# One ScalarE copy for a head's eight transposed blocks instead of two, and TensorE waiting for the whole of it

## The chip, the cores and the metric

The kernel runs on one core of a Trainium2 chip. The metric is the device time of one launch in microseconds; smaller is better. One core has five engines that run their own instruction streams in order and meet only at semaphores: TensorE (PE, with PEld for its weight loads), VectorE (DVE), ScalarE (ACT), GpSimd (POOL) and SyncE (SP), which issues the DMAs.

## The reference

A four-stage layer stack on `x` of shape (8, 1024, 256), in float32. The change touches the first stage alone:

```python
def _L0_attn_ref(hidden_states, ...):          # on layernorm(x); H = 16 heads of hd = 16
    q = (x @ Wq.T + bq).reshape(b, s, h, hd)   # k, v alike
    attn_scores = jnp.einsum('bihd,bjhd->bhij', q, k) / scale
    li = x @ rel_W[:, :d].T
    lj = x @ rel_W[:, d:].T
    relation_probs = jax.nn.softmax(li[:, :, None, :] + lj[:, None, :, :] + rel_b, axis=-1)
    bias = jnp.einsum('bijk,hk->bhij', relation_probs, logical_bias)
    attn_scores = attn_scores + gate * bias
    attn_weights = jax.nn.softmax(attn_scores, axis=-1)
    out = jnp.einsum('bhij,bjhd->bihd', attn_weights, v).reshape(b, s, d)
    return out @ Wo.T + bo
```

The three stages behind it (a matrix product with fp8 weights, a Mamba block with its scan and MLP, a gated FFN) are not touched.

## The kernel before

Attention goes over 64 tiles of 128 queries (8 batches of 8 tiles, `TILES`), and in each tile over 16 heads (`H`). It takes place from about 200 us to about 3470 us of the trace. The order on every engine is written out by hand: each engine has a `body` that runs once for a tile `t`, with a loop over `u` = 0..15 inside. A semaphore that counts heads uses `U = 16 t + h`.

For head `u` of a tile the steps are these.

- `dve_f` (L315, twelve heads) or `pool_f` (L225, L227; heads 4, 8, 12 and 15) builds the relation bias of the head in one of eight row buffers `srow`.
- `pe_s` (L469) computes the 128x1024 scores into PSUM (`ps_s`, one buffer). It waits until VectorE is done with the head before (`s_ok`).
- `dve_s` (L326) adds bias and scores, leaves the result in `srow`, and finds the row's extremum; it gives `s_ok`.
- `act_e` (L398) takes the exponential of the 128x1024 row on ScalarE.
- `pe_t` (L480) transposes the eight 128x128 blocks of the head `u - 2` (`LAG` is 2) into PSUM tile `ps_t`, which has two halves of four blocks: 2 KB each for a partition, 4 KB together, and no second buffer.
- `act_at` (L407) copies `ps_t` into `AT` in SBUF, in two instructions of 128x512, one for each half.
- `pe_pv` (L492) multiplies `AT` with the values, for groups of four heads, in three pieces at u % 4 = 3, 0 and 1.

The wait pairs around `ps_t` go by halves. TensorE may write half 0 of the next head as soon as half 0 of this one has been copied, and ScalarE may copy half 0 as soon as four transposes are done.

Beside the heads, a tile carries the work of its neighbours at fixed places of the loop over `u`. On ScalarE in `body`: after the copy of u = 1, 4 and 5 the exponentials of the next tile's relation terms (`act_rel`, L381 and L385), at u = 5 `act_o` (L411, the output accumulator for `pe_oT`), at u = 7 `act_gate` (L375), at u = 8 `act_xT` (L345), at u = 9 `act_y0` (L391, a logarithm, and L393, an exponential of its result), at u = 11 `act_d` (L349, L352), at u = 15 `act_p` (L361). The output of `act_y0` goes to GpSimd (`pool_t`, L212), and its result to VectorE (`dve_y`, L303) at u = 11, which sits in VectorE's queue ahead of the heads 12 to 15. On TensorE at u = 5 there is `pe_v` (L457), at u = 6 `pe_oT` (L502; VectorE's `dve_norm`, L332, waits for it), at u = 7 `pe_xT` (L427), at u = 9 `pe_d` (L444), at u = 10 `pe_g` (L450).

In what follows T(h) is the eight transposes of head h, copy(h) the copy or the two copies of `act_at` for head h, and exp(u) the exponential of `act_e`. At step u ScalarE issues exp(u), copy(u - 2), and then the extra work; TensorE issues the scores of head u + 1, T(u - 2), the piece of `pe_pv`, and then the extra work.

Of the kernel before, what the change touches and what calls it, by code (L numbers as in the profile page):

```python
# [21 lines left out]
H = 16  # L22
HD = D // H
HG = 4
# [7 lines left out]
def wait(eng, sem, value):  # L32

    if isinstance(value, int) and value <= 0:
        return
    eng.wait_ge(sem, value)
# [10 lines left out]
def attention(nc, x_in, wqk, wvg, bqk, rows, ident_in, parts_d, x_out):  # L47
# [6 lines left out]
    NROW = 8  # L54
# [6 lines left out]
    NAT = 2 * HG  # L61
    with ExitStack() as ctx:
# [54 lines left out]
        AT = [sb(f"AT{i}", [P, NT, P]) for i in range(NAT)]  # L117
# [9 lines left out]
        ps_t = psum("ps_t", [P, 2, HG, P])  # L127
# [45 lines left out]
        t_ok = sem("t_ok")  # L173
# [227 lines left out]
        def act_at(act, t, h):  # L401
            U = H * t + h
            if h % HG == 0:
                wait(act, pv_ok, U // HG + 1 if isinstance(U, int) else HG * t + h // HG + 1)
            for half in range(2):
                wait(act, t_ok, 2 * NROW + 2 * U + half + 1)
                nc.scalar.copy(AT[h % NAT][:, HG * half:HG * half + HG, :], ps_t[:, half]).then_inc(at_ok, 1)  # L407

        def act_o(act, o):
            wait(act, pv_ok, 2 + HG * (o + 1))  # L410
# [62 lines left out]
        def pe_t(pe, t, h):  # L473
            U = H * t + h
            wait(pe, e_ok, U + 1)
            for half in range(2):
                wait(pe, at_ok, 2 * U + half + 1)
                for i in range(HG):
                    j = HG * half + i
                    last = nc.tensor.transpose(ps_t[:, half, i, :], rows_sb[h % NROW][:, j * P:(j + 1) * P], ident[:])  # L480
                last.then_inc(t_ok, 1)

        def pe_pv(pe, t, par, j, blocks):
            if blocks[0] == 0:
                if j == 0:
                    wait(pe, o_ok, t)
                    wait(pe, v_ok, 2 + NT * (t // NT + 1))
                wait(pe, at_ok, 2 + 2 * (H * t + HG * j + HG))
            for n in blocks:
                for i in range(HG):  # L490
                    h = HG * j + i
                    last = nc.tensor.matmul(ps_o[32 * i:32 * i + 32, j, :], V[par][:, n, h, :],  # L492
                                            AT[h % NAT][:, n, :], start=(n == 0), stop=(n == NT - 1))
            if blocks[-1] == NT - 1:
                last.then_inc(pv_ok, 1)
# [316 lines left out]
        @block.scalar  # L812
        def _(act):
            def front(act, p):
                act_xT(act, p)
                act_d(act, p)
                act_hi(act, p)
                act_mid(act, p)

            def project(act, p, k, par, ib):  # L820
                act_xT(act, p)
                act_d(act, p)
                act_hi(act, p)
                act_gate(act, p, par, ib)
                act_mid(act, p)

            def start(act):
                front(act, NT)
                for step in range(3):
                    act_rel(act, 0, 0, step)  # L830
                act_y0(act, 0)
                act_p(act, 0, 0)

            def body(act, t, k, par, ib, pro, post, look, before):
                for u in range(H):
                    act_e(act, t, u)
                    if u >= LAG:
                        act_at(act, t, u - LAG)
                    elif post:
                        act_at(act, t - 1, H + u - LAG)  # L840
                    if followed(t, pro) and u == 0:
                        act_hi(act, t - 1 + AHEAD)
                    if u == 0 and (not isinstance(t, int) or t >= 2):
                        act_aT(act, t - 2)
                    if look and u in (1, 4, 5):
                        act_rel(act, t + 1, 1 - k, (1, 4, 5).index(u))
                    if followed(t, pro) and u == 3:
                        act_mid(act, t - 1 + AHEAD)
                    if post and u == 5:
                        act_o(act, t - 1)  # L850
                    if pro and u == 7:
                        act_gate(act, t + NT, 1 - par, ib)
                    if pro and u == 8:
                        act_xT(act, t + AHEAD)
                    if look and u == 9:
                        act_y0(act, t + 1)
                    if pro and u == 11:
                        act_d(act, t + AHEAD)
                    if look and u == 15:
                        act_p(act, t + 1, 1 - k)  # L860

            def finish(act):
                for u in range(H - LAG, H):
                    act_at(act, TILES - 1, u)
                act_aT(act, TILES - 2)
                act_o(act, TILES - 1)
                act_aT(act, TILES - 1)

            act.preload_act_table_set("natural_log_exp_and_others")
            act.sem_inc(at_ok, 2)  # L870
            run(act, start, project, body, finish)

        @block.tensor
# [1018 lines left out]
```

## Time and profile before

| | us |
|---|---|
| median of 3 runs | 7194.83 |
| the runs | 7194.24 to 7202.27 |
| the profiled execution | 7195.28 |
| its span in the trace | 7193.3 |
| TensorE busy | 5460.0 (76%) |
| VectorE busy | 5274.5 (73%) |
| ScalarE busy | 3797.2 (53%) |
| GpSimd busy | 4038.8 (56%) |

The span runs from the first to the last instruction of the trace; 2.0 us of the execution lie around it. The busy shares are means over four stages with different limits, so for the change only the attention stage counts. The page's slices are 180 us each; attention fills the second to the nineteenth.

### The profile page before, as it was taken

What the parts mean: (1) busy time and instruction counts of PE and PEld (TensorE: products, weight loads), DVE (VectorE), ACT (ScalarE), POOL (GpSimd) and SP (SyncE); (2) the same over time, 40 slices, a digit from 0 to 9 for tenths busy, and PEclk for the clock granted to TensorE, in tenths of its full rate; (3) what the DMA queues carried; (4) which work ended last, traced back from release to release, by engine and by line L of the source; (5) the groups of instructions that cost most, each with busy time, mean ns of one, the idle gap of its engine ahead of it and who ended that gap; (6) DMA issues with size and microseconds to landing.
All of it is one profiled execution on the core that took longest, in us unless ns stands there. A gap on an engine that the chain in (4) does not pass through costs nothing. (4 is left out here: it accounts for less than half of the span.)

```text
span 7193.3 us, 118342 instructions
## 1 busy us (share of the span) xinstructions
PE 5460.0 (76%) x36898; PEld 3382.9 (47%) x36898; DVE 5274.5 (73%) x6522; ACT 3797.2 (53%) x5385; POOL 4038.8 (56%) x2175
## 2 busy tenths in 40 slices
PE   4688888888888888877535667667666666999999
PEld 3466565656665665655322222222222223666665
DVE  1788888888888888888776998998988986121221
ACT  1788888888888888888313333333333332111111
POOL 2777676767776777766223766866865864000000
PEclk7899999999999999999767988888888888999999
DMA  1212121110212021110223343443443434101110
GB/s 36 35 28 40 27 41 26 35 32 23 44 24 44 23 43 24 29 30 14 68 97 108 140 144 118 149 138 120 147 144 112 155 132 136 44 29 44 29 44 9
DMA packets 401678, 486.09 MB, mean 68 GB/s; under 512 B 225936, under 2 KB 303504, under 8 KB 401184
## 3 DMA queue, kind: packets, MB, share of 16 engines
q1 hardware_dynamic: 401184, 479.68, 22.9%
q8 instruction: 289, 4.73, 0.3%
q14 instruction: 205, 1.68, 0.1%
HBM read 394.25 MB, written 85.33 MB: 67 GB/s over the span
## 5 line engine op out<-in xcount | busy, mean ns | idle before, releaser
L1391 PE MATMUL c_ps_y<-c_hc,c_ident 128*128 128x512 f32 x2048 | 1127.3, 698 | 680.8 <-POOL c_hc L1417 326.4
L326 DVE CUSTOM_DVE_ANT_0 srow<-srow,ps_s,cur 128x1024 f32<-128x1024 f32 x1024 | 1304.8, 1274 | 317.3 <-PE ps_s L469 271.2
L1410 POOL TENSOR_TENSOR c_db<-c_conv,c_bs 128x1024 f32<-128x1024 f32 x512 | 1221.6, 2415 | 502.1 <-DVE c_conv L1536 411.1
L398 ACT ACTIVATE srow<-srow,nmax 128x1024 f32<-128x1024 f32 x1024 | 1186.6, 1159 | 279.8 <-DVE nmax L326 269.4
L407 ACT COPY AT<-ps_t 128x512 f32<-128x512 f32 x2048 | 1110.6, 594 | 248.4 <-PE ps_t L480 246.6
L1445 ACT ACTIVATE c_pd<-c_dt,c_a_neg 128x1024 f32<-128x1024 f32 x512 | 571.6, 1117 | 1140.4 <-DVE c_hc L1555 1011.1
L480 PE MATMUL ps_t<-ident,srow 128*128 128x128 f32 x8192 | 1136.4, 284 | 18.0 <-ACT AT L407 17.6
L480 PEld LDWEIGHTS ps_t<-ident,srow 128*128 128x128 f32 x8192 | 1000.5, 146 | 279.3 <-ACT AT L407 68.7
L469 PE MATMUL ps_s<-K,Q 96*128 96x512 bf16 x2048 | 645.9, 398 | 602.0 <-DVE nmax L326 519.0
L1391 PEld LDWEIGHTS c_ps_y<-c_hc,c_ident 128*128 128x128 f32 x2048 | 423.5, 220 | 1389.8 <-issue 510.8
L1546 DVE TENSOR_TENSOR_SCAN c_pd<-c_pd,c_db 128x1024 f32<-128x1024 f32 x384 | 876.5, 2283 | 0.0
L315 DVE SCALAR_TENSOR_TENSOR srow<-ps_p,rho,R 128x1024 f32<-128x1024 f32 x640 | 817.9, 1278 | 0.8 <-ACT ps_p L361 0.8
L227 POOL TENSOR_TENSOR srow<-srow,R 128x1024 f32<-128x1024 f32 x256 | 642.4, 2509 | 47.0 <-POOL srow L225 47.0
L492 PE MATMUL ps_o<-AT,V 128*32 128x128 f32 x16384 | 660.2, 295 | 0.0
L469 PEld LDWEIGHTS ps_s<-K,Q 96*128 96x128 bf16 x2048 | 145.1, 99 | 801.7 <-DVE nmax L326 687.8
L1694 POOL TENSOR_TENSOR d_rstd<-d_ve,d_mhalf 128x4 f32<-128x4 f32 x16 | 16.3, 1019 | 898.7 <-DVE d_ve L967 898.7
L492 PEld LDWEIGHTS ps_o<-AT,V 128*32 128x32 f32 x16384 | 433.8, 116 | 146.6 <-issue 141.6
L1555 DVE TENSOR_TENSOR c_hc<-c_pd,c_cs 128x1024 f32<-128x1024 f32 x384 | 470.1, 1224 | 13.3
L1417 POOL TENSOR_TENSOR c_hc<-c_hs,c_cs 128x1024 f32<-128x1024 f32 x128 | 300.1, 2344 | 183.4 <-DVE c_hs L1546 182.4
L200 POOL TENSOR_TENSOR R<-Dj,RT 128x1024 f32<-128x1024 f32 x128 | 300.7, 2371 | 101.3 <-DVE RT L298 101.3
L217 POOL TENSOR_TENSOR R<-R,R 128x1024 f32<-128x1024 f32 x128 | 300.4, 2367 | 92.1 <-DVE R L303 92.1
L1721 DVE TENSOR_TENSOR d_x<-d_ps_y,d_y 128x512 f32<-128x512 f32 x32 | 22.1, 692 | 438.3 <-PE d_ps_y L1796 438.3
(180 smaller groups left out, 8166.3 us busy)
## 6 DMA issues: line engine op xcount, KB each, us to landing
c_bs<-bc_rows_d SPq DMA_DIRECT2D x256, 512.0 KB, 4.8
c_cs<-bc_rows_d SPq DMA_DIRECT2D x256, 512.0 KB, 4.1
parts_d<-parts SPq DMA_DIRECT2D x65, 384.0 KB, 3.3
K<-parts_d SPq DMA_DIRECT2D x192, 128.0 KB, 4.5
Q<-parts_d SPq DMA_DIRECT2D x384, 64.0 KB, 2.9
ym_d<-c_conv SPq DMA_DIRECT2D x32, 512.0 KB, 2.9
d_ym<-ym_d SPq DMA_DIRECT2D x16, 1024.0 KB, 7.3
xt<-in_x SPq DMA_DIRECT2D x65, 128.0 KB, 3.2
```

Source lines behind the costliest of these rows:

```text
L227: nc.gpsimd.tensor_tensor(r[:], r[:], R[k][0][:], ALU.add).then_inc(fp_ok, 1)
L315: nc.vector.scalar_tensor_tensor(r[:], p1[:], rho[:, h:h + 1], R[k][0][:], ALU.mult, ALU.add).then_inc(fd_ok, 1)
L326: nc.vector.tensor_tensor_reduce(r[:], r[:], ps_s[:], cur[k][:, h:h + 1], BIG, ALU.add, ALU.min, nmax[:, h % NROW:h % NROW + 1]).then_inc( ...
L398: nc.scalar.activation(r[:], r[:], ACT.Exp, scale=-1.0, bias=nmax[:, h % NROW:h % NROW + 1]).then_inc(e_ok, 1)
L407: nc.scalar.copy(AT[h % NAT][:, HG * half:HG * half + HG, :], ps_t[:, half]).then_inc(at_ok, 1)
L469: last = nc.tensor.matmul(ps_s[:, n * 512:(n + 1) * 512], Q6[k][:, h, :], K6[:, h, n * 512:(n + 1) * 512], start=True, stop=True)
L480: last = nc.tensor.transpose(ps_t[:, half, i, :], rows_sb[h % NROW][:, j * P:(j + 1) * P], ident[:])
L492: last = nc.tensor.matmul(ps_o[32 * i:32 * i + 32, j, :], V[par][:, n, h, :], AT[h % NAT][:, n, :], start=(n == 0), stop=(n == NT - 1))
L1391: last = nc.tensor.matmul(ps_y[:, c, cut], ident[:], hc[(2 * n + c) % RING][:, cut], start=n == 0, stop=n == NS - 1)
L1410: nc.gpsimd.tensor_tensor(db[(2 * n + c) % RING][:], conv[:, 2 * pair + c, :], bs[n % RING][:], ALU.mult).then_inc(db_ok, 1)
L1445: nc.scalar.activation(pd[:, c, :], dt[:, m, :], ACT.Exp, scale=a_neg[:, m, n:n + 1]).then_inc(da_ok, 1)
L1546: nc.vector.tensor_tensor_scan(h, pd[:, c, :], db[(2 * n + c) % RING][:], 0.0, ALU.mult, ALU.add).then_inc(h_ok, 1)
```

## The change

ScalarE waits for all eight transposes of a head and copies them with one instruction of 128x1024, where it had two waits and two instructions of 128x512. The semaphore `at_ok` goes up by one for a head where it went up by two. TensorE waits, ahead of the eight transposes of a head, until the whole copy of the head before it is done; before, it waited for half 0 ahead of the first four and for half 1 ahead of the last four. The initial value of `at_ok` and the wait of `pe_pv` are renumbered to match.

```diff
@@ act_at
-            for half in range(2):
-                wait(act, t_ok, 2 * NROW + 2 * U + half + 1)
-                nc.scalar.copy(AT[h % NAT][:, HG * half:HG * half + HG, :], ps_t[:, half]).then_inc(at_ok, 1)
+            wait(act, t_ok, 2 * NROW + 2 * U + 2)
+            nc.scalar.copy(AT[h % NAT][:], ps_t[:].rearrange("p a i t -> p (a i) t")).then_inc(at_ok, 1)
@@ pe_t
             wait(pe, e_ok, U + 1)
+            wait(pe, at_ok, U + 1)
             for half in range(2):
-                wait(pe, at_ok, 2 * U + half + 1)
                 for i in range(HG):
@@ pe_pv
-                wait(pe, at_ok, 2 + 2 * (H * t + HG * j + HG))
+                wait(pe, at_ok, 1 + H * t + HG * j + HG)
@@ block.scalar
-            act.sem_inc(at_ok, 2)
+            act.sem_inc(at_ok, 1)
```

## Rows read from the trace of the kernel before

**Rows 1.** The page: busy time of each engine over the whole span.

```profile
PE 5460.0 (76%) x36898; PEld 3382.9 (47%) x36898; DVE 5274.5 (73%) x6522; ACT 3797.2 (53%) x5385; POOL 4038.8 (56%) x2175
```

**Rows 2.** Busy by windows: from:to us, length, engines, clock, DMA share, GB/s.

```profile
1000.00:1600.00 600.00, 488.27 (x5414) 357.11 (x5416) 504.28 (x708) 499.10 (x748) 430.44 (x257) 0.94 0.17 35
```

**Rows 3.** Waits of 1200 to 1800 us: waiting engine, line, releaser, total us, times, longest.

```profile
DVE srow L326 <- PE ps_s L469: 54.0, 38, 3.1
ACT AT L407 <- PE ps_t L480: 52.0, 53, 3.6
...
PEld ps_t L480 <- ACT AT L407: 13.6, 24, 0.7
```

**Rows 4.** Line L303, whole span: ns min/median/max, and its idle time before.

```profile
L303 DVE SCALAR_TENSOR_TENSOR R<-RT,R x64: 1224/1226/1227, 203.0 to 3403.5; 128x1024 f32<-128x1024 f32 x64
...
  POOL RT L212: 130.4, 64
```

**Rows 5.** Lines L407 and L361, whole span, and who waited for L407.

```profile
L407 ACT COPY AT<-ps_t x2048: 562/589/692, 223.4 to 3459.8; 128x512 f32<-128x512 f32 x187
...
  PEld ps_t L480: 68.7, 116
...
L361 ACT COPY ps_p<-R x64: 1016/1036/1037, 209.0 to 3417.7; 128x1024 f32<-128x1024 f32 x64
```

**Rows 6.** Timeline, a head whose copy waits: start us, us, engine, line, [idle before].

```profile
1504.49 1.04 PE L480 MATMUL ps_t<-ident,srow 128*128 128x128 f32 x8
...
1505.13 1.07 ACT L407 COPY AT<-ps_t 128x512 f32<-128x512 f32 x2 [0.80 <-PE ps_t L480]
```

**Rows 7.** Timeline, the same tile, from T(2) to T(5).

```profile
1509.15 1.01 PEld L480 LDWEIGHTS ps_t<-ident,srow 128*128 128x128 f32 x8
1509.36 1.04 PE L480 MATMUL ps_t<-ident,srow 128*128 128x128 f32 x8
...
1510.00 1.07 ACT L407 COPY AT<-ps_t 128x512 f32<-128x512 f32 x2
...
1510.96 1.16 ACT L385 ACTIVATE R<-R,cur 128x1024 f32<-128x1024 f32 x1
...
1515.05 0.60 ACT L411 COPY O<-ps_o 128x512 f32<-128x512 f32 x1
...
1516.57 1.09 ACT L407 COPY AT<-ps_t 128x512 f32<-128x512 f32 x2
...
1517.22 0.91 PEld L480 LDWEIGHTS ps_t<-ident,srow 128*128 128x128 f32 x8 [0.66 <-ACT AT L407]
```

**Rows 8.** Timeline, the same tile, from copy(5) to `dve_y`.

```profile
1518.56 1.11 ACT L407 COPY AT<-ps_t 128x512 f32<-128x512 f32 x2
...
1519.73 0.11 PEld L469 LDWEIGHTS ps_s<-K,Q 96*128 96x128 bf16 x2 [0.44 <-DVE nmax L326]
...
1519.96 1.01 PEld L480 LDWEIGHTS ps_t<-ident,srow 128*128 128x128 f32 x8
...
1522.35 1.01 PEld L480 LDWEIGHTS ps_t<-ident,srow 128*128 128x128 f32 x8
...
1523.20 1.08 ACT L407 COPY AT<-ps_t 128x512 f32<-128x512 f32 x2
...
1524.16 1.07 ACT L391 ACTIVATE R<-RT 128x1024 f32<-128x1024 f32 x1
...
1526.51 2.37 POOL L212 TENSOR_TENSOR RT<-RT,R 128x1024 f32<-128x1024 f32 x1 [1.60 <-ACT R L393]
...
1528.92 1.23 DVE L303 SCALAR_TENSOR_TENSOR R<-RT,R 128x1024 f32<-128x1024 f32 x1 [1.74 <-POOL RT L212]
```

**Rows 9.** Timeline, a tile of the last batch: T(5), and the first half of `act_y0`.

```profile
3248.17 0.91 PEld L480 LDWEIGHTS ps_t<-ident,srow 128*128 128x128 f32 x8 [0.85 <-ACT AT L407]
...
3255.01 1.07 ACT L391 ACTIVATE R<-RT 128x1024 f32<-128x1024 f32 x1
```

**Rows 10.** Timeline, the end of the same tile as Rows 7, heads 12 and 13 on ScalarE.

```profile
1532.57 1.15 ACT L398 ACTIVATE srow<-srow,nmax 128x1024 f32<-128x1024 f32 x1 [1.43 <-DVE nmax L326]
```

## The prediction

> **What bounds the kernel now.** I read the page first: no engine is busy for more than 76% of the span [rows 1], so the stage has to be read by itself. In a window inside attention TensorE, VectorE, ScalarE and GpSimd are busy for 488, 504, 499 and 430 of 600 us [rows 2]: 81, 84, 83 and 72%. None is full; what sets a tile's time is a chain that passes from engine to engine. The waits say where: over 12 tiles VectorE waits 54.0 us for scores [rows 3]. The view of the line L303 (`dve_y`) shows the other place, and that it is there in every tile: 64 of its 64 instructions came after idle time of VectorE that ended with GpSimd's L212, 130.4 us in all, 2.0 us each [rows 4]. In the timeline L212 in turn sat idle for 1.60 us until ScalarE's L393, the second half of `act_y0`, and the first half, L391, starts on ScalarE with no idle time before it, right behind copy(7) [rows 8]. So one point of ScalarE's queue is on the path of every tile: if ScalarE is late at L391 (u = 9), L212 is late, `dve_y` is late, and so are heads 12 to 15 and the next tile behind it. What has to be found out is how late the change makes L391.
>
> **The change, part by part.** First the prices.
>
> (a) The copy itself. A pair of 128x512 copies that runs without a pause takes 1.07 us, the second starting 0.48 after the first; one lasts 589 ns [rows 5, 6]. A single ScalarE copy of 128x1024 is in the trace only with PSUM on its output side: L361, 1016 ns at least and 1036 at the median [rows 5]. For one that reads PSUM over two halves there is no row. Bounds: 1.02 us, L361's shortest, and 1.18, twice 589 ns, if nothing overlapped. I take 1.03, next to L361's median, since it has the same width and the same two memories. Behind a pair the next instruction starts 0.11 before the end (1510.00 + 1.07 against 1510.96) [rows 7]; so the fused copy takes up 0.92 us of the queue for the pair's 0.96. ScalarE gains about 0.04 us for a head (at the upper bound it loses 0.11).
>
> (b) The later start. Where ScalarE is ready first, the pair starts 0.64 us after the first transpose (1504.49 to 1505.13) [rows 6]. The fused copy needs all eight, which end 1.04 us after that start; with the 0.04 that a semaphore takes, 1.08. It starts 0.44 later and ends 0.40 later. Where ScalarE is more than 0.44 us behind TensorE, this costs nothing.
>
> (c) The later release of `ps_t`. TensorE could load for T(h+1) when half 0 of copy(h) was done, 0.59 us after the start; now at 1.03: 0.44 later. Before, this wait decided in two places of a tile (T(5) and T(9)): 24 waits in 12 tiles, 13.6 us [rows 3], 116 waits in the whole span [rows 5].
>
> (b) and (c) close a ring: 0.21 us from the weight load of T(h) to its first transpose (1509.15 to 1509.36) [rows 7], 1.08 to the copy, 1.03 for the copy, 0.06 to the next weight load (1516.57 + 0.59 = 1517.16 against 1517.22) [rows 7]. 2.38 us for a head, and no other engine can shorten it. The heads in the middle of a tile follow each other at 2.39 us (1519.96 to 1522.35) [rows 8]. By itself the ring doesn't slow them, but it has no reserve: a lag that gets into it stays until a head with slack.
>
> (d) The waits that fall out, one for a head on each of the two engines, I cost at nothing: the second copy followed the first at the width of its data, so the wait had been hidden under it. No DMA is moved, and nothing in SP's queue waits for `at_ok` or `t_ok`. Queued behind TensorE's wait are a piece of `pe_pv`, the extra work and the scores of a later head; behind ScalarE's, its extra work and the next exponential. VectorE's and GpSimd's builders of the bias wait for the transposes of a head eight earlier, which leaves them heads of slack.
>
> Now one tile with these prices.
> 1. copy(2): 1509.36 + 1.08 = 1510.44; exp(4) in front of it, pushed by the later copy(1), ends 0.06 after that. 1510.50 for 1510.00 [rows 7], +0.50; behind it +0.46.
> 2. From there to copy(4) ScalarE is full (L385, exp(5), copy(3), L385, L411, exp(6)), and copy(3) gives back its 0.04: L411 starts 0.44 later [rows 7]. `pe_oT` and `dve_norm` behind it come 0.3 to 0.4 later, and VectorE with them.
> 3. copy(4): 1517.01 for 1516.57, done 1518.04; T(5) is loaded at 1518.10 for 1517.22 [rows 7]: +0.88, half the lag, half (c).
> 4. copy(5): 1518.10 + 0.21 + 1.08 = 1519.39 for 1518.56 [rows 8]: +0.83. By the ring T(6) can be loaded at 1520.48. TensorE's own work from T(5) to T(6) was 2.74 us (1517.22 to 1519.96), 0.44 of it idle ahead of the scores [rows 8]; 2.30, and with some 0.2 of short pauses between weight loads that the idle time hid, 2.5: T(6) at 1520.60 for 1519.96, +0.64.
> 5. T(7) by the ring: 1522.98 for 1522.35 [rows 8], +0.63. copy(7): 1522.98 + 1.29 = 1524.27 for 1523.20, +1.07.
> 6. L391 follows 0.92 later: 1525.19 for 1524.16, +1.03. L212 and `dve_y` wait for it and nothing else [rows 8], so `dve_y` comes 1.03 us later. VectorE's own lateness there (head 11's scores stand behind T(7), 0.64) is covered by its 1.74 us of idle time in front of L303 [rows 8].
> 7. Behind `dve_y`, ScalarE sits idle for 1.43 us before exp(12) [rows 10]: the ring starts empty, and copies that end 0.40 later end in idle time. Nothing is added, and nothing is given back, since the next tile starts from VectorE.
>
> Tiles of the last batch have no projection work, yet T(5) waits for ScalarE there too (0.85 us) and L391 has no idle time before it [rows 9]; the same walk gives about the same. `act_y0` of a next tile is in 63 tiles: 63 x 1.03 = 65 us. Outside attention nothing changes. The profiled execution has 7195.28 us (span 7193.3 and 2.0 around it), 0.45 over the median; so 7260.3 beside it, and against the median **7260 us**, +0.9%.
>
> In heads like that of [rows 6] ScalarE waits 0.80 us for the transposes, and the split lets it begin at the half. The Trainium skill, page "Perfetto Trace Analysis", section "Optimizing Scalar/DVE Operations", has a rule for either side: grouping into larger operations improves throughput if the engine is saturated, and breaking up instructions may let work complete sooner where an unsaturated Scalar or Vector engine causes bubbles on others. By its first half the result would be A below, by its second the forecast.
>
> **The rivals.**
> A. *ScalarE's queue alone decides at L391, and the merger shortens it: faster.* For it: ScalarE has no idle time from copy(2) to L391. If it is always more than 0.44 us behind TensorE, copies 2 to 7 give back 0.04 us each, 0.24 a tile, 15 us: 7180; if a pair really used 2 x 0.59 us, 0.15 each, 0.9 a tile, 57 us: 7138. Against it: ScalarE waited for the transposes 53 times in 12 tiles [rows 3], and T(5) for the copy.
> B. *Covered.* The 2.0 us in front of `dve_y` take the lag: 7195. Against it: that idle time ends with the chain from L391; it is no slack of the chain.
> C. *The copy is at its upper bound.* At 1.18 each of copies 2 to 7 adds 0.15, 0.9, less the 0.1 that TensorE's own work hides at T(6): 1.83 a tile, 115 us: 7310.
> D. *Every head pays (b)*: 16 x 0.44 x 64 = 451 us: 7646. It would need the ring to be slower than VectorE's pace in all heads; [rows 8] and [rows 10] speak against that. In the Trainium skill "Perfetto Trace Analysis", section "Optimizing Tensor Performance", advises that independent matmul groups rotate through PSUM banks so that copying one out overlaps the next; taken for every head it points to D.
> E. *The lag is caught at heads 6 and 7* (TensorE's pauses rearrange), and L391 is late only by (b), 0.40: 25 us, 7220.
>
> **How the numbers follow.** Forecast 0.54, C 0.15, E 0.13, D 0.02, A 0.09, B 0.07. The range reaches from a little under E, 7212, to a little over C, 7315; outside are A, B and D, 0.18. A measurement of this kernel can't tell less than 0.2%, 14 us, from no change. Slower by more: 0.54 + 0.15 + 0.13 + 0.02 = 0.84; within: 0.07; faster: 0.09.
>
> **What would show it.** L407 1024 times at about 1.03 us; TensorE's waits for L407 in more heads than two a tile, over 1 us at T(5) in place of 0.66; weight loads of T(5), T(6), T(7) at least 2.38 us apart; L391 with no idle time before it, and 1 us later counted from copy(2) less its own 0.5; L303's mean idle time 0.4 longer, still ended by L212; the tiles, now (3417.7 - 209.0) / 63 = 50.9 us apart by L361 [rows 5], 51.9 apart. L407 at 1.1 or more would be C; L391 with idle time before it, or L303 released by something else, would make the chain wrong; a wait of TensorE for L407 in nearly every head, D.

## The result and the profile after

The changed kernel took 7261.03 us at the median of 4 runs (7255.17 to 7269.7), the kernel before 7194.53 beside it (7191.02 to 7202.27). The ratio is 1.0092 [1.0077, 1.0107]: slower by 66.5 us (55 to 77). The forecast of 7260 was met, but partly by luck: the tile itself lost less than predicted, and its borders lost time that the prediction had at nothing.

The profiled execution of after took 7269.7 us, 8.7 over its median. In its code every line behind L405 has a number one smaller: the copy is L406, the transposes are L479, the scores L468, `act_o` L410.

The page of after: the span, the busy time of each engine ([rows 1] of before), and two groups of its list (busy time and mean ns, then the idle time in front and who ended most of it).

```profile
span 7267.8 us, 115462 instructions
...
PE 5450.7 (75%) x36898; PEld 3379.3 (46%) x36898; DVE 5293.4 (73%) x6522; ACT 3739.0 (51%) x4361; POOL 4050.1 (56%) x2175
...
L406 ACT COPY AT<-ps_t 128x1024 f32<-128x1024 f32 x1024 | 1035.3, 1011 | 462.8 <-PE ps_t L479 456.4
L479 PE MATMUL ps_t<-ident,srow 128*128 128x128 f32 x8192 | 1137.5, 284 | 131.0 <-ACT AT L406 115.5
```

ScalarE has 1024 instructions less and is busy 58 us less, and the kernel is slower. The work that the change saved was done by an engine that waits; the waits grew by more.

The views of single lines of after. For L406: ns min/median/max, its idle time before, and who waited for it. For L303 (`dve_y`) and L361 (`act_p`) the same, cut to what answers to [rows 4] and [rows 5].

```profile
L406 ACT COPY AT<-ps_t x1024: 989/1012/1027, 224.4 to 3526.2; 128x1024 f32<-128x1024 f32 x171
...
  PE ps_t L479: 456.4, 675
...
  PE ps_t L479: 115.5, 139
```

```profile
L303 DVE SCALAR_TENSOR_TENSOR R<-RT,R x64: 1224/1225/1227, 203.0 to 3466.8; 128x1024 f32<-128x1024 f32 x64
...
  POOL RT L212: 152.8, 64
...
L361 ACT COPY ps_p<-R x64: 1017/1022/1023, 209.1 to 3482.6; 128x1024 f32<-128x1024 f32 x64
```

By L361 the tiles are now (3482.6 - 209.1) / 63 = 51.96 us apart, 1.03 more than before [rows 5]. L303 waits for L212 in 64 of 64 tiles as before, 2.39 us each in place of 2.04 [rows 4].

The timeline of after, in the tile of [rows 6 to 8] (start us, us, engine, line, and the idle time before in brackets). In before, VectorE's L326 for head 3 of this tile starts at 1504.85, in after at 1527.99; shifts below are counted from there.

```profile
1527.99 1.28 DVE L326 CUSTOM_DVE_ANT_0 srow<-srow,ps_s,cur 128x1024 f32<-128x1024 f32 x1 [0.81 <-PE ps_s L468]
...
1533.58 1.01 ACT L406 COPY AT<-ps_t 128x1024 f32<-128x1024 f32 x1
...
1538.53 0.58 ACT L410 COPY O<-ps_o 128x512 f32<-128x512 f32 x1
...
1540.04 1.01 ACT L406 COPY AT<-ps_t 128x1024 f32<-128x1024 f32 x1
...
1541.17 0.86 PEld L479 LDWEIGHTS ps_t<-ident,srow 128*128 128x128 f32 x8 [1.25 <-issue]
1541.20 1.06 PE L479 MATMUL ps_t<-ident,srow 128*128 128x128 f32 x8 [0.78 <-ACT AT L406]
...
1542.30 1.01 ACT L406 COPY AT<-ps_t 128x1024 f32<-128x1024 f32 x1 [0.19 <-PE ps_t L479]
...
1543.48 1.01 PEld L479 LDWEIGHTS ps_t<-ident,srow 128*128 128x128 f32 x8
...
1545.90 0.92 PEld L479 LDWEIGHTS ps_t<-ident,srow 128*128 128x128 f32 x8 [0.21 <-issue]
...
1547.10 1.01 ACT L406 COPY AT<-ps_t 128x1024 f32<-128x1024 f32 x1
...
1548.00 1.06 ACT L391 ACTIVATE R<-RT 128x1024 f32<-128x1024 f32 x1
...
1550.34 2.35 POOL L212 TENSOR_TENSOR RT<-RT,R 128x1024 f32<-128x1024 f32 x1 [1.97 <-ACT R L393]
...
1552.73 1.23 DVE L303 SCALAR_TENSOR_TENSOR R<-RT,R 128x1024 f32<-128x1024 f32 x1 [2.10 <-POOL RT L212]
...
1555.07 1.27 DVE L326 CUSTOM_DVE_ANT_0 srow<-srow,ps_s,cur 128x1024 f32<-128x1024 f32 x1
```

The chain of the prediction is all there: L391 right behind copy(7), L212 behind L393, L303 behind L212, and head 12 right behind L303. From head 3 to head 12 it took 27.08 us (1555.07 - 1527.99), in before 26.41.

That distance is the measure for all that follows. It starts behind the disturbances of the tile's border and ends behind `dve_y`, and it hardly differs between most tiles. With the rest of the tile, read in the same way from the starts of L326 (over the tiles 1 to 55, from head 3 to head 12 the median and for the other stretches the mean; "attention" is from the first L326 to the last, and the first L326 lies some 212 us behind the start of the span):

| us | before | after | difference |
|---|---|---|---|
| head 3 to head 12 | 26.41 | 27.08 | +0.67 |
| head 12 to head 15 | 9.84 | 9.68 | -0.16 |
| head 15 to head 3 of the next tile | 15.01 | 15.46 | +0.45 |
| attention, whole | 3241.4 | 3306.1 | +64.7 |
| behind attention | 3739.7 | 3749.3 | +9.6 |

So 63 x 0.67 = 42 us come from the tile and 63 x 0.29 = 18 us from its border (heads 12 to 3). Added up over all tiles it is 44.4 and 20.4 us: the first tile of all alone lost 2.6 from head 3 to head 12 (26.37 to 29.00), and the borders of the last batch, which the means leave out, lost 4.3 (there head 3 to head 12 went from 26.27 to 26.96, much as elsewhere). The 9.6 us behind attention are in code that the change doesn't touch; over the 14 profiles of this study that part has between 3739.6 and 3749.3 us, for reasons that stay open, and the two medians differ by 66.5, not by the 74.4 of the two profiled executions.

All such distances come from one profiled execution of each kernel, and executions of one kernel lie up to 20 us apart. The distance from head 3 to head 12 comes out alike over 55 tiles. A border figure is softer: 10 us in the total would be 0.16 us a tile.

### The profile page after: what moved, and what is told of

It reads as the page before. It is cut to its first block and busy times, and to the rows that moved or that the text cites. A ratio compares the mean times of both kernels' runs of the same rounds, so it can differ in the third digit from the quotient of the medians.

```text
span 7267.8 us, 115462 instructions
## 1 busy us (share of the span) xinstructions
PE 5450.7 (75%) x36898; PEld 3379.3 (46%) x36898; DVE 5293.4 (73%) x6522; ACT 3739.0 (51%) x4361; POOL 4050.1 (56%) x2175
## 5 line engine op out<-in xcount | busy, mean ns | idle before, releaser
L326 DVE CUSTOM_DVE_ANT_0 srow<-srow,ps_s,cur 128x1024 f32<-128x1024 f32 x1024 | 1303.9, 1273 | 339.5 <-PE ps_s L468 269.9
L406 ACT COPY AT<-ps_t 128x1024 f32<-128x1024 f32 x1024 | 1035.3, 1011 | 462.8 <-PE ps_t L479 456.4
L479 PE MATMUL ps_t<-ident,srow 128*128 128x128 f32 x8192 | 1137.5, 284 | 131.0 <-ACT AT L406 115.5
L479 PEld LDWEIGHTS ps_t<-ident,srow 128*128 128x128 f32 x8192 | 998.9, 147 | 403.1 <-issue 252.3
L468 PE MATMUL ps_s<-K,Q 96*128 96x512 bf16 x2048 | 641.6, 396 | 553.0 <-DVE nmax L326 453.1
L315 DVE SCALAR_TENSOR_TENSOR srow<-ps_p,rho,R 128x1024 f32<-128x1024 f32 x640 | 816.9, 1276 | 2.6 <-ACT ps_p L361 2.6
L227 POOL TENSOR_TENSOR srow<-srow,R 128x1024 f32<-128x1024 f32 x256 | 647.2, 2528 | 47.0 <-POOL srow L225 47.0
L468 PEld LDWEIGHTS ps_s<-K,Q 96*128 96x128 bf16 x2048 | 149.1, 99 | 735.1 <-DVE nmax L326 610.6
```

What stands on the lines that cost most here:

```text
L227: nc.gpsimd.tensor_tensor(r[:], r[:], R[k][0][:], ALU.add).then_inc(fp_ok, 1)
L315: nc.vector.scalar_tensor_tensor(r[:], p1[:], rho[:, h:h + 1], R[k][0][:], ALU.mult, ALU.add).then_inc(fd_ok, 1)
L326: nc.vector.tensor_tensor_reduce(r[:], r[:], ps_s[:], cur[k][:, h:h + 1], BIG, ALU.add, ALU.min, nmax[:, h % NROW:h % NROW + 1]).then_inc( ...
L406: nc.scalar.copy(AT[h % NAT][:], ps_t[:].rearrange("p a i t -> p (a i) t")).then_inc(at_ok, 1)
L468: last = nc.tensor.matmul(ps_s[:, n * 512:(n + 1) * 512], Q6[k][:, h, :], K6[:, h, n * 512:(n + 1) * 512], start=True, stop=True)
```

## The experiments

All edits are against the kernel before unless it says otherwise. A run of before on the same chip stands beside each: 7194.59 us for the first four, 7197.05 for the next four, 7197.65 for the last four.

### 1 to 3. Which of the two waits costs, with two copies kept

The change has three parts: ScalarE starts when all eight transposes are done (b), TensorE starts when the whole copy is done (c), and two copies are merged into one (a). Three kernels take (b) alone, (c) alone, and both, each with two copies of 128x512.

```diff
# e1_act_whole, in act_at
             for half in range(2):
-                wait(act, t_ok, 2 * NROW + 2 * U + half + 1)
+                if half == 0:
+                    wait(act, t_ok, 2 * NROW + 2 * U + 2)
# e2_pe_whole, in pe_t
             for half in range(2):
-                wait(pe, at_ok, 2 * U + half + 1)
+                if half == 0:
+                    wait(pe, at_ok, 2 * U + 2)
# e3_both_two_copies: both
```

ScalarE's wait alone:

> ScalarE waits for all eight transposes of a head, but still copies in two instructions; TensorE still waits by halves. Theory (the chain through L391): the later start alone makes L391 about 0.4 us later in a tile, 63 x 0.4 = 25 us over the kernel before, about 7220, and the in-tile part of the loss is about half of that of the changed kernel. Rival (TensorE's longer wait for the whole copy is the cost): no more than 5 us over before, 7195 to 7200.

TensorE's wait alone:

> TensorE waits for the whole copy of the head before it ahead of the eight transposes; ScalarE starts at the half and copies in two instructions, as before. Theory (the chain through L391): T(5) and T(9) are loaded 0.4 us later, the 0.44 us TensorE idles ahead of the scores takes it, L391 hardly moves: 7195 to 7202. Rival (TensorE's wait is the cost): 7225 to 7260.

Both:

> Both waits are for the whole, as in the changed kernel, but the copy is still two instructions of 128x512. Theory: the merger itself is a small gain (0.05 us for a head in ScalarE's queue, and as much in the ring), so this is slower than the changed kernel by about 0.3 us a tile: 7270 to 7285. Rival (something in the one wide copy, or in the shorter instruction stream, costs): as fast as or faster than the changed kernel, 7261 or less.

| kernel | median us (range) | ratio to before | head 3 to 12 | 12 to next 3 | attention |
|---|---|---|---|---|---|
| (b) alone | 7268.98 (7264.48 to 7271.23) | 1.0103 [1.0087, 1.0118] | 27.26 | 25.05 | 3306.6 |
| (c) alone | 7207.43 (7201.82 to 7214.76) | 1.002 [1.0011, 1.0029] | 26.40 | 24.87 | 3241.5 |
| both, two copies | 7266.22 (7261.53 to 7273.1) | 1.0101 [1.0085, 1.0116] | 27.26 | 25.01 | 3307.0 |

The same tile in the timelines, first of (b) alone, then of (c) alone: head 3 and head 12 on VectorE, and L391 between them.

```profile
1528.88 1.28 DVE L326 CUSTOM_DVE_ANT_0 srow<-srow,ps_s,cur 128x1024 f32<-128x1024 f32 x1 [0.92 <-PE ps_s L470]
...
1549.07 1.07 ACT L391 ACTIVATE R<-RT 128x1024 f32<-128x1024 f32 x1
...
1556.14 1.27 DVE L326 CUSTOM_DVE_ANT_0 srow<-srow,ps_s,cur 128x1024 f32<-128x1024 f32 x1
```

```profile
1502.25 1.28 DVE L326 CUSTOM_DVE_ANT_0 srow<-srow,ps_s,cur 128x1024 f32<-128x1024 f32 x1 [0.18 <-issue]
...
1521.56 1.07 ACT L391 ACTIVATE R<-RT 128x1024 f32<-128x1024 f32 x1
...
1528.65 1.27 DVE L326 CUSTOM_DVE_ANT_0 srow<-srow,ps_s,cur 128x1024 f32<-128x1024 f32 x1
```

L391 starts 20.19 us behind head 3 in the first and 19.31 in the second; in before it was 19.31 (1524.16 [rows 8] - 1504.85). So (c) moves nothing at L391, though TensorE did wait longer for the copy. From 1200 to 1800 us, the wait of (c) alone that answers to the last line of [rows 3] is

```profile
PEld ps_t L481 <- ACT AT L407: 25.2, 24, 1.1
```

as often as before and 11.6 us more, 0.48 each. That is the size of the prediction's (c), 0.44. It is gone at the next head: counted from head 3, the weight loads of T(5), T(6) and T(7) start at 12.86, 15.17 and 17.50 us, in before at 12.37, 15.11 and 17.50. With (b) in place, (c) adds nothing either: 27.26 with and without it.

The merger is the difference of after and "both, two copies": 27.08 - 27.26 = -0.18 us a tile, 11 us in 63 tiles, for copies 2 to 7, where 6 x 0.04 = 0.24 was predicted. The medians of the two differ by 5.2 us in the same direction, with ranges that overlap, and attention by 0.9 us: most of what the tile gave back went at the borders.

The times met none of the three expectations. (b) alone costs 74 us, three times the 25 expected (experiments 11 and 12 say why in the tile). Both with two copies came out 4 us below the expected range. And (c) alone, though it is free from head 3 to head 12 and its profiled attention is as long as in before, is 12.8 us slower at the median, clear of the noise and above the 7195 to 7202 expected. Its profiled execution, 7202.24, was one of its fastest, and has its extra time behind attention (3746.2 us for 3739.7). Where the rest of the 12.8 us lies isn't shown.

The Trainium skill, page "Perfetto Trace Analysis", section "Optimizing Scalar/DVE Operations", has a rule for each of these two numbers: larger operations help a saturated engine, and broken-up ones let work complete sooner where an unsaturated engine causes bubbles on others. Both effects exist here, and the second is nearly five times the first: +0.85 a tile for the whole start, -0.18 for the merger.

### 4 and 5. Take L391 off the place behind copy(7)

If the path goes through ScalarE's queue at L391, then L391 issued ahead of copy(7) should give the tile back about one copy, with either kernel.

```diff
# e4_after_y0_early (against after), e5_before_y0_early (against before)
                     act_e(act, t, u)
+                    if look and u == 9:
+                        act_y0(act, t + 1)
...
-                    if look and u == 9:
-                        act_y0(act, t + 1)
```

After, with it:

> The changed kernel with the two instructions of act_y0 (L391, L393) issued ahead of copy(7) instead of behind it. Theory (the tile's length hangs on L391): L391 starts about 1 us earlier, dve_y too, and the copy of head 7 has slack: 63 x 0.7 to 1.0 us faster than the changed kernel, 7198 to 7217. Rival (the cost is in the transposes, their copies and what stands behind them on TensorE): no gain or a loss, since copy(7) comes 2 us later: 7261 or more.

Before, with it:

> The kernel before (two copies, waits by halves) with the two instructions of act_y0 (L391, L393) issued ahead of copy(7) instead of behind it. Theory (the tile's length hangs on L391): L391 starts 0.9 us earlier in every tile and head 12 on VectorE with it, 63 x 0.9 = 57 us less than before, 7138 to 7150. Rival (the gain of the same move in the changed kernel only took back what the change had cost, because the idle time in front of dve_y has another floor): 7185 to 7195.

| kernel | median us (range) | ratio to before | head 3 to 12 | 12 to next 3 | attention |
|---|---|---|---|---|---|
| after, L391 early | 7194.85 (7187.06 to 7207.45) | 0.9997 [0.9988, 1.0006] | 26.07 | 25.08 | 3234.9 |
| before, L391 early | 7117.46 (7109.62 to 7125.41) | 0.9892 [0.9877, 0.9907] | 25.36 | 24.43 | 3153.8 |

The same tile in before with L391 early:

```profile
1467.04 1.28 DVE L326 CUSTOM_DVE_ANT_0 srow<-srow,ps_s,cur 128x1024 f32<-128x1024 f32 x1 [0.18 <-issue]
...
1485.34 1.04 ACT L391 ACTIVATE R<-RT 128x1024 f32<-128x1024 f32 x1
...
1490.06 1.22 DVE L303 SCALAR_TENSOR_TENSOR R<-RT,R 128x1024 f32<-128x1024 f32 x1 [0.69 <-POOL RT L212]
...
1492.39 1.27 DVE L326 CUSTOM_DVE_ANT_0 srow<-srow,ps_s,cur 128x1024 f32<-128x1024 f32 x1
```

L391 starts 18.30 behind head 3, 1.01 earlier than in before, and head 12 comes 7.05 behind L391, in before 7.10 (1531.26 - 1524.16). The idle time ahead of `dve_y` fell from 1.74 [rows 8] to 0.69. This makes the rule for what a tile costs from head 3 to head 12: L391's place plus 7.05 to 7.09, at the median of every kernel here. It also makes the change's price at L391 independent of what follows copy(7): after less before with L391 early is 0.71 (26.07 - 25.36), and 0.67 without. Before gained 79.6 us at the median and 87.6 in its attention (3241.4 to 3153.8); 1.05 x 63 = 66 are this, the rest comes from the borders, 24.43 for 24.85 (nothing in the last batch). Both kernels came out below the expected range, after by 3 us and before by 21: the expectation for before had 0.9 us a tile and nothing at the borders.

### 6 and 7. The border, and the loop's jump

The border was worse by 0.29 us a tile in after, which nothing in the prediction allows for. The clearest difference there is at tile 28, the fifth of its batch, where TensorE's loop over two tiles has just jumped back to its start. The timeline of after, the weight loads of TensorE for two heads of that tile:

```profile
1675.29 0.11 PEld L468 LDWEIGHTS ps_s<-K,Q 96*128 96x128 bf16 x2 [3.67 <-issue]
...
1678.27 1.57 PEld L479 LDWEIGHTS ps_t<-ident,srow 128*128 128x128 f32 x8 [2.87 <-issue]
```

"issue" means that the engine waited for nothing that the trace shows. In before the same place has

```profile
1650.10 0.11 PEld L469 LDWEIGHTS ps_s<-K,Q 96*128 96x128 bf16 x2 [3.24 <-DVE nmax L326]
```

So TensorE was idle there too, but VectorE's head was as late, and the pause was hidden. To test whether the jump makes it, the loop over the pairs of tiles of a batch is written out, in before and in after (for the first seven batches; the last has a loop of its own, which stays):

```diff
-                with eng.Fori(1, NT // 2 - ends) as i:
+                for i in range(1, NT // 2 - ends):
```

Before, written out:

> The kernel before with the six inner tiles of each batch written out instead of a loop of two tiles, on all engines; the order of the work is the same. Theory (the uneven part of the changed kernel's loss, about 20 us, is TensorE waiting for its instructions at the jump back of the loop): fewer jumps, 7170 to 7195, and the tiles of one position in the batch get alike. Rival (the pauses come with every new stretch of code, jump or not): 7195 or more, as many pauses as before.

After, written out:

> The changed kernel, unrolled in the same way. Theory (0.67 us in every tile from ScalarE's queue, and the rest from pauses at the jump): 42 us over the unrolled kernel before, not 66; about 7215 to 7235. Rival (the whole 66 us come from the waits themselves): 60 to 70 us over the unrolled kernel before.

| kernel | median us (range) | ratio to before | head 3 to 12 | 12 to next 3 | attention |
|---|---|---|---|---|---|
| before, written out | 7189.54 (7180.0 to 7195.79) | 0.999 [0.9981, 0.9999] | 26.39 | 24.74 | 3232.9 |
| after, written out | 7218.21 (7208.59 to 7220.02) | 1.0029 [1.0018, 1.0039] | 27.08 | 24.20 | 3251.8 |

The waits of TensorE ahead of the scores that ended with nothing but issue, from 230 to 3450 us (total us, times, longest), in before, in after, in before written out and in after written out:

```profile
PE ps_s L469 <- issue: 38.3, 10, 6.0
```

```profile
PE ps_s L468 <- issue: 56.2, 14, 7.0
```

```profile
PE ps_s L469 <- issue: 13.5, 3, 5.7
```

```profile
PE ps_s L468 <- issue: 13.2, 3, 5.4
```

10 pauses in before and 14 in after become 3 and 3. Every one of them lies ahead of the second head of a tile that follows a jump back, and the three that are left lie behind the jumps that are left: two of the outer loop over pairs of batches (tiles 24 and 40) and one of the last batch's own loop (tile 60). The jump makes the pauses; what happens in one, the trace doesn't tell. How long it holds up the scores depends on where VectorE is: behind the end of VectorE's head before them, the scores of u = 1 and 2 start 1.71 and 1.31 us late at the fifth tile of a batch in before, 3.29 and 2.58 in after, and under 0.1 in both when written out (means over seven batches).

The border, from head 12 to head 3 of the tile named, in the first seven batches, means in us, shows what that costs:

| kernel | into the fifth tile | into the seventh | into the second to fourth, sixth and eighth |
|---|---|---|---|
| before | 24.89 | 24.81 | 24.69 |
| after | 27.08 | 26.09 | 24.44 |
| before, written out | 24.54 | 24.66 | 24.65 |
| after, written out | 24.24 | 23.96 | 24.09 |

The fifth and the seventh tile are those behind an inner jump. The 14 borders into them are 24.3 us longer in after than in before, the others together 8 us shorter: all that the border lost lies at the jump. (A pause that shows isn't a loss by itself: (c) alone has 25.50 and 26.44 us there, 24.32 in the last column, and the mean of before.) After therefore pays more for the same jump, and it gains more by losing it: 43 us against 8 (7261.03 less 7218.21, 7197.05 less 7189.54).

But it gains too much. With the in-tile price unchanged (+0.69, 43 us in 63 tiles), attention is only 18.9 us longer in the one written-out kernel than in the other, and the medians are 28.7 apart, where 42 was expected: now after's border is the shorter, by 0.54 us, and not at the jump alone. (The profiled execution of before written out lies 5.7 us above its median and that of after written out 9.6 below, so the 18.9 says too little.) There is a second thing at the border. VectorE builds the bias of heads 0 and 1 from SBUF (L315 with `R` as its input), and the mean time of that instruction differs. The groups of before, after, before written out and after written out, in this order (busy us, mean ns):

```profile
L315 DVE SCALAR_TENSOR_TENSOR srow<-R,rho,R 128x1024 f32<-128x1024 f32 x128 | 265.4, 2074 | 9.5 <-POOL R L217 4.9 <-issue 4.6
```

```profile
L315 DVE SCALAR_TENSOR_TENSOR srow<-R,rho,R 128x1024 f32<-128x1024 f32 x128 | 258.0, 2017 | 9.7 <-POOL R L217 4.9 <-issue 4.8
```

```profile
L315 DVE SCALAR_TENSOR_TENSOR srow<-R,rho,R 128x1024 f32<-128x1024 f32 x128 | 312.6, 2443 | 8.0 <-POOL R L217 4.8 <-issue 2.4 <-PE ps_t L480 0.8
```

```profile
L315 DVE SCALAR_TENSOR_TENSOR srow<-R,rho,R 128x1024 f32<-128x1024 f32 x128 | 189.7, 1483 | 9.4 <-POOL R L217 4.9 <-issue 4.5
```

Beside L227 on GpSimd one of them takes 1.27 or 2.9 us, by which of the two starts first. In after written out L315 is ahead by 0.14 us, and L227 takes 3.36; in before L227 is ahead by 0.61, takes 2.39, and L315 takes 2.87:

```profile
1491.73 1.27 DVE L315 SCALAR_TENSOR_TENSOR srow<-R,rho,R 128x1024 f32<-128x1024 f32 x1
1491.87 3.36 POOL L227 TENSOR_TENSOR srow<-srow,R 128x1024 f32<-128x1024 f32 x1 [0.18 <-POOL srow L225]
```

```profile
1490.63 2.39 POOL L227 TENSOR_TENSOR srow<-srow,R 128x1024 f32<-128x1024 f32 x1 [0.18 <-POOL srow L225]
1491.24 2.87 DVE L315 SCALAR_TENSOR_TENSOR srow<-R,rho,R 128x1024 f32<-128x1024 f32 x1
```

The border thus has two forms, and small shifts choose. Over 2.5 us are 86 of the 128 in before written out and 10 in after written out. But this doesn't set the border's length by itself: before with L391 early has 116 of 128 over 2.5 us, 2801 ns on average, and one of the shorter borders (24.43).

### 8 to 10. Both edits together, and the fused copy where nothing waits for it

Before with L391 early and the loop written out is the fastest that these findings point to; after with the same two edits shows what the change costs when jump and queue place are out of the way; and before with both, with a fused copy for heads 3 and 5 alone, uses the merger where ScalarE is behind TensorE anyway.

```diff
# e9_best_fused_3_5, in act_at, beside both edits
+            if h in (3, 5):
+                wait(act, t_ok, 2 * NROW + 2 * U + 2)
+                nc.scalar.copy(AT[h % NAT][:], ps_t[:].rearrange("p a i t -> p (a i) t")).then_inc(at_ok, 2)
+                return
```

Before with both:

> Both edits on the kernel before: act_y0 ahead of copy(7), and the six inner tiles of a batch written out. Theory: the two gains are in different places of a tile and add up, 7115 to 7145. Rival: the longer stretch of code costs what the earlier act_y0 gives, 7195.

After with both:

> The changed kernel with act_y0 ahead of copy(7) and the six inner tiles of a batch written out. Theory: the lag at the scores of head 12 is 0.7 us over the kernel before with the same two edits (7092), 45 us by that alone, and what the unrolled changed kernel won back at the tiles' borders (13 us of 42) may come again: 7120 to 7140. Rival (with act_y0 out of the way the changed kernel's later copies have nothing left to delay): 7092 to 7100.

Before with both and two fused copies:

> The kernel before with act_y0 ahead of copy(7) and the six inner tiles written out (7092), and with the one wide copy at heads 3 and 5 alone, where ScalarE is over 0.44 us behind the transposes and TensorE comes to the next head after the copy's end. Theory (one wide copy costs nothing there and shortens ScalarE's queue by 0.05 us each): 0.1 us less from head 3 to head 12, 6 us, 7084 to 7092. Rival (no gain, the queue's time is set by what it waits for): 7092 to 7098.

| kernel | median us (range) | ratio to before | head 3 to 12 | 12 to next 3 | attention |
|---|---|---|---|---|---|
| before, both edits | 7092.41 (7091.44 to 7098.03) | 0.9859 [0.9844, 0.9874] | 25.36 | 24.16 | 3139.4 |
| after, both edits | 7181.19 (7171.1 to 7189.18) | 0.9977 [0.9966, 0.9987] | 26.08 | 24.85 | 3222.0 |
| before, both, two fused | 7092.11 (7091.12 to 7104.33) | 0.986 [0.9843, 0.9876] | 25.30 | 24.23 | 3138.4 |

Before with both edits is 104.6 us faster than before, more than the 79.6 and 7.5 of the edits one by one, and 23 below the expected range; where the extra 17 come from isn't shown. After with both edits missed its expectation by 41 us. It is 88.8 us behind before with both, and its attention is 82.6 longer: added up over the tiles, 43 from head 3 to head 12, as in every pair, and 40 at the borders (0.69 a tile), where I had expected the price of the tile alone. With the jumps gone, this isn't the jump's. One sign is again VectorE beside GpSimd, here L298 beside L190. The groups from 230 to 3100 us of before with both and of after with both:

```profile
L298 DVE SCALAR_TENSOR_TENSOR RT<-Dj,cur,RT 128x1024 f32<-128x1024 f32 x58 | 88.7, 1529 | 0.0
```

```profile
L298 DVE SCALAR_TENSOR_TENSOR RT<-Dj,cur,RT 128x1024 f32<-128x1024 f32 x56 | 103.7, 1853 | 0.0
```

That is 0.3 us a tile of the 0.69. What picks the border's form in a given kernel stays open.

The two fused copies give 0.06 us a tile, 4 us (0.1 and 6 us expected), which the times can't resolve (7092.11 against 7092.41). Even where it is put with care, the merger is worth next to nothing here.

### 11 and 12. Where the later start enters

In (b) alone the tile lost 0.85 us, twice the 0.44 by which one copy starts later. The walk of the prediction says that a lag of 0.46 is carried from copy(2) and that the copies behind the waits of T(5) to T(7) add theirs. So the whole wait was put to head 2 alone, and to heads 6 and 7 alone (the same edit with `(6, 7)`).

```diff
             for half in range(2):
-                wait(act, t_ok, 2 * NROW + 2 * U + half + 1)
+                if h not in (2,):
+                    wait(act, t_ok, 2 * NROW + 2 * U + half + 1)
+                elif half == 0:
+                    wait(act, t_ok, 2 * NROW + 2 * U + 2)
```

> The kernel before, but ScalarE waits for all eight transposes at one head of a tile alone, head 2 (copy(2)). Theory (the lag enters ScalarE's full stretch at copy(2), stays to L391, and passes through L411 to VectorE): from the scores of head 3 to those of head 12 VectorE takes 0.43 us more, 63 x 0.43 = 27 us, 7215 to 7230. Rival (0.44 us in one head is swallowed by the idle time in front of dve_y): 26.41 us from head 3 to head 12 as before, 7195.

> The kernel before, but ScalarE waits for all eight transposes at heads 6 and 7 of a tile alone. Theory (the later start enters a second time here, because copy(6) and copy(7) follow their own transposes with no lag to hide in): 0.44 us more from head 3 to head 12, 28 us, 7215 to 7230, and with the run of head 2 the 0.85 us of the kernel in which ScalarE waits for all at every head. Rival (the two heads pay one after the other): 0.88 us and 55 us, or nothing.

| kernel | median us (range) | ratio to before | head 3 to 12 | 12 to next 3 | attention |
|---|---|---|---|---|---|
| head 2 | 7233.89 (7229.26 to 7235.12) | 1.0051 [1.0034, 1.0067] | 26.84 | 24.98 | 3273.3 |
| heads 6 and 7 | 7233.14 (7231.03 to 7238.06) | 1.0051 [1.0034, 1.0068] | 26.83 | 25.04 | 3274.2 |

+0.43 and +0.42, and together the +0.85 of all heads. The later start counts once at each end of the stretch in which ScalarE is full: where it enters it, and where it follows its own transposes again. Since the two make up the whole, the heads between don't pay, and neither do the other heads on the way to head 12. The border differs again (+0.13 and +0.19 a tile), so attention is 32 and 33 us longer (3273.3 and 3274.2 for 3241.4) and not 27; the medians lost 36 and 35, 4 and 3 us over the expected range.

## Why the prediction was right, and where it wasn't

**The chain** held at every point read: L391 has no idle time before it, L212 waits for L393, L303 for L212, and the moved L391 shows that this is what the time hangs on.

**(a) The copy.** 1012 ns at the median, between the bounds and near the 1.03 taken; L391 starts 0.90 behind it (1548.00 - 1547.10), where 0.92 was used. The merger gave 0.18 a tile for 0.24. The Trainium skill, page "ScalarE: Activation LUTs", section "What ACT_TABLE_LOAD costs", gives an ACTIVATE with immediate operands 186 ns and 0.833 ns an element: by estimate, if the copy counts as one, 1039 ns for 1024 elements and 612 for 512. This case measured 1012 and 589, and the measurement decides.

**(b) The later start.** 0.44 was right, and so was that it enters twice. In the tile it is the whole price of the change.

**(c) The later release** was right as a wait (0.48 at T(5)) and wrong on the path: it adds nothing at L391. Both of the walk's steps that carried it on, 4 and 5, are too large. What (c) alone costs at the median, 12.8 us, has no place in the walk.

**The walk** has a small slip of its own: behind copy(2) it had 0.46, copy(3) gives back 0.04, and it went on with 0.44, not 0.42. Step by step, with the predicted shift behind each measured one: copy(2) +0.44 (+0.50); L410 +0.34 (+0.44), since copies 2 and 3 gave back 0.05 each; copy(4) +0.33; T(5) +0.81 (+0.88); copy(5) +0.60 (+0.83); T(6) +0.38 (+0.64); T(7) +0.41 (+0.63); copy(7) +0.76 (+1.07); L391 +0.70 (+1.03); `dve_y` +0.67 (+1.03).

The term that was mis-sized is the ring in (b) and (c). It took 0.21 us from the weight load of T(h) to its first transpose, read at T(2), where TensorE comes out of other work [rows 7]. Where TensorE has waited for the copy, the first transpose follows its load by 0.03 (1541.17 and 1541.20), the copy starts 1.10 behind that and takes 1.01, and 0.12 later the next load can go (1541.17 behind the end of copy(4) at 1541.05): 2.26 us, not 2.38. That is also the shortest distance between the loads of two heads anywhere in after. The ring had 0.13 us of reserve at the pace of 2.39, where the prediction said none. The loads of T(5) and T(6) in after are 2.31 apart, under the minimum that I had given. So the lag of T(5) was caught by T(6), and T(6) and T(7) come later only as much as VectorE does, 0.3 to 0.4: the lag that went through L410, `pe_oT` and `dve_norm` in step 2. From there on, copy(7) adds its own later start.

**Step 7**, "nothing is added, and nothing is given back", failed. From head 12 to head 3 of the next tile after lost another 0.29 us a tile, 18 us. The jump of TensorE's loop is shown as the place: the borders behind an inner jump are 24.3 us longer, the others 8 shorter, and written out the excess is gone. Why the pause hits after harder, and why the other borders differ from kernel to kernel (by up to 0.7 us a tile between kernels without inner jumps), is not shown; the two forms of the border exist and differ, but don't explain the lengths. That the total came out within 1 us of the forecast was luck, the sum of two errors of opposite sign: 65 - 42 = 23 too much in the tile and 24 too little outside it.

**The signs.** Right: the copy's count and duration, 1.25 us of idle time ahead of T(5)'s loads (over 1 said), L303 waiting 0.35 longer for L212 (0.4 said), tiles 51.96 apart (51.9, by the same luck as the total), 139 waits of TensorE for the copy in 64 tiles, about two a tile as before, so not the every-head case D. Wrong: TensorE's waits in more heads than two a tile; loads at least 2.38 apart; L391 a whole 1 us later (0.70).

**The rivals.** B (covered) and A (faster) are excluded by the result and experiments 1 to 5, C by the copy's 1012 ns. E, with L391 late by 0.40 alone, would be the truth for (b) at one end of the full stretch only (experiments 11 and 12). The advice to rotate PSUM banks, from the page "Perfetto Trace Analysis" of the Trainium skill, section "Optimizing Tensor Performance", was weighed for D: this `ps_t` has no second buffer, and giving up the use of its halves by TensorE cost nothing from head 3 to head 12 (experiment 2).

## What to carry to other kernels

When two instructions are merged, price first what waits for their input: the merged one starts later by the time in which the other half is produced, wherever its engine was ahead, and that weighs more than the fixed cost saved (here 0.85 against 0.18 us a tile, with 58 us less of busy time on ScalarE and 66 us more in total). A delay in a ring of engines counts only at the points where the ring is the last to arrive, so read the ring's own minimum from a place where it did wait, not from one where it didn't. And look for the instruction on the path that stands in a queue behind one that isn't: moving L391 ahead of one copy was worth 80 us, more than the change cost.

## What the runs showed of the hardware beyond that

**TensorE's granted clock at the borders.** The windows of before, in the tile ahead of the one read above (from:to us, length, busy us of PE, PEld, DVE, ACT and POOL, then the granted clock):

```profile
1495.00:1497.00 2.00, 1.64 (x16) 1.26 (x20) 1.62 (x5) 1.66 (x3) 0.00 (x0) 0.94 0.00 0
1497.00:1502.00 5.00, 4.31 (x42) 2.99 (x38) 5.00 (x6) 3.30 (x7) 2.33 (x2) 0.50 0.00 0
...
1504.00:1510.00 6.00, 4.89 (x54) 3.58 (x52) 5.15 (x8) 5.17 (x8) 3.00 (x3) 1.00 0.08 25
```

and TensorE's rows in before: the idle time ahead of that fall, and the eight transposes of a head at a granted clock of 1.00 and of 0.50:

```profile
1495.36 0.11 PEld L469 LDWEIGHTS ps_s<-K,Q 96*128 96x128 bf16 x2 [2.44 <-DVE nmax L326]
...
1495.81 1.04 PE L480 MATMUL ps_t<-ident,srow 128*128 128x128 f32 x8
...
1650.74 1.91 PE L480 MATMUL ps_t<-ident,srow 128*128 128x128 f32 x8
```

TensorE was idle for 2.44 us, went on, and then ran at 0.50, its level of 1.2 GHz, until about 1503.6; eight transposes take 1.91 us there for 1.04. In attention, before spends 397 us at the lower level in 86 stretches and after 389 in 90, so the change didn't lose its time by more of it. With L391 early, before has 294 us in 65 stretches. Those that begin at heads 12 and 13 fall from 34 to 2, those that begin at head 15 rise from 2 to 30. That may be part of the gain at the border; no run separates it.

**The loop's jump** goes with a pause of TensorE ahead of its second head: 3.3 to 4.9 us at the inner loop's jump, 5.9 to 7.0 at the outer one's, where it wasn't hidden by VectorE being later (before and after; experiments 6 and 7).

**VectorE beside GpSimd.** A `scalar_tensor_tensor` of 128x1024 with both inputs in SBUF (L315) takes 1.28 us alone and 2.9 where it starts behind L227 on GpSimd; where it starts ahead of L227 it keeps 1.27, and L227 takes 3.36 for 2.4. Its variant that reads `ps_p` in PSUM keeps 1.28 throughout. In one and the same program the order changes from tile to tile.
